# A two-layer graph network on one core: edge values in a ring, twelve gather buffers instead of eight, and some loads issued from another queue

## The chip, the core and the metric

The kernel runs on one core of one Trainium2 chip. The core has five engines that run their own instruction streams and meet at semaphores: TensorE (PE, matmuls; its weight loads are listed as PEld), VectorE (DVE), ScalarE (ACT), GpSimd (POOL) and SyncE (SP), which here only issues DMAs. ACT, SP and POOL can each issue DMAs; each has a queue of its own (SPq, ACTq and POOLq in the rows). Time is device microseconds of one execution, the median of several.

## The reference

1250 nodes with 512 features, 40000 edges sorted by destination. Layer 0 sums over typed edges, layer 1 is a normalised graph convolution:

```
h = relu(layernorm(x))
weight = einsum('rb,bio->rio', w_comp, bases)      # 32 types, 8 bases
msg = (h @ weight[type])[src] * edge_weight
x = x + segment_sum(msg, dst) + h_bias
h = relu(layernorm(x))
h = h @ W.T + b
x = x + relu(segment_sum(norm * h[row], col))      # with self loops, norm from degrees
```

## The kernel before

**Tiles.** The destinations fall into 20 tiles of 64 nodes (NTI), taken in pairs in a fixed order (TORDER). The edges of a tile are cut into slots of 128; there are SL = 335 slots. Of slot s the kernel needs the 128 source rows, two fp16 parts of 512 values and 128 more columns that help count edges (ROW = 1152 values, 2304 bytes a row). They are gathered from a table in HBM (rows_layer0), which the setup writes.

**Gathers.** POOL issues one indirect DMA per slot (line 722) into one of UN = 8 buffers (gath). From slot 8 on it waits for s_used: PE has finished slot s-8. Before slot 5 it waits once for s_cols, since setup values of DVE lie in the later buffers.

**Edge values.** For each edge eight values are needed (its weight times w_comp of its type, one per base). They are made in 42 groups of 8 slots (VB). SP loads the types of a group as rows (line 579, four small DMAs, a ring of three buffers), DVE turns them into a one-hot tile (one_hot_types, line 1087), PE looks the values up (look, line 1404), DVE adds and scales (lines 1094, 1098), ACT casts the high half into val (val_hi, line 782), DVE subtracts the low half (line 1104). All 336 slots have their own place in val. For batches of up to four slots (BATCHES) DVE then spreads the values over the destination window (select, lines 1141 to 1147), in a ring of three batches (sel).

**PE.** For each slot PE runs twelve narrow matmuls (edges, line 1501) into four PSUM banks of a tile and one for the counts (line 1507), which ends the slot and raises s_used. When a tile is done, ACT and DVE flush it (lines 830, 1225, 833) to fp16 parts and PE may not start the next tile's banks before. When both tiles of a pair are flushed, PE has 96 matmuls of 512 columns with the split bases (product, line 1521), then a transpose (turn, line 1530) and a projection with W1 (project, line 1541). After the last slot follow the last products and layer 1's aggregation (line 1595).

**What sets the order.** All engines walk the same list of slots. STEPS[s] says what other work stands behind slot s. PROD[s] says which product matmuls do; they are put between the narrow ones of the next slot. PROD comes from a planner (place_products) that adds up modelled times of gathers, of PE and of the wait for a free buffer, s - UN, and gives each slot some products, 14 where a tile ends, so that they are there to run while the flush goes on.

**The setup.** The bases (8 of 1 MB), W1 (1 MB) and the biases are loaded by SP. ACT squares each base and W1 as they land (squares_of, line 797), for a bound: STEPS puts bases 5 to 7 and W1 behind slots 0 to 3. Behind slot 7 PE transposes the sums (columns_of(1), line 1376), DVE makes the scales from them (scales), and from slot 10 on ACT and DVE split one base every three slots (split_base, lines 841 and 1261). SP's order here is: bases 0 to 4, table rows (line 594), types of groups 0 to 2, bases 5 to 7 (line 558), the two biases (600, 601), W1 (626), types of groups 3 to 5, and x (623).

A general path for inputs that aren't sorted stands in If blocks on each engine; it isn't run here.

## Time and profile before

| | us |
|---|---|
| median of 3 runs | 630.19 (628.79 to 630.42) |
| span of the profiled execution | 625.8 |
| median minus span | 4.4 |

| engine | busy us | share of the span | instructions |
|---|---|---|---|
| PE | 496.4 | 79% | 5824 |
| PEld | 317.0 | 51% | 5824 |
| DVE | 328.6 | 52% | 929 |
| ACT | 151.9 | 24% | 272 |
| POOL | 352.2 | 56% | 473 |

The profile gives one execution, instruction by instruction, from the first to the last instruction of any engine; that is the span. A time of its own around the span isn't given for that execution, so the span is set beside the median. In the slices each digit is a share in tenths. "PEclk" is the clock granted to PE, as a share of 2.4 GHz; its other level is 1.2 GHz. In the order of time a row gives start, duration, engine, line, operation and tiles, and in brackets how long the engine idled before it and what ended that. A matmul's busy time overlaps its neighbours', since their ends are modelled. Names of tiles are those of the memory, so where setup values lie in another tile's place, the row names that tile: base loads go to room_b, W1 to u_t.

### The profile page before, as it was taken

To read this page: it belongs to the slowest core of one execution; us is meant where nothing else is said; L and a number is where in the kernel's file an instruction comes from. 1 tells how busy PE (TensorE), PEld (TensorE's weight loads), DVE (VectorE), ACT (ScalarE), POOL (GpSimd) and SP (SyncE) were. 2 spreads that over 40 slices of the span, in tenths; PEclk is the share of its full clock that TensorE was granted. 3 is DMA by queue.
4 is the path that set the end of the run, shared out by engine and by line. 5 is a ranking of instruction groups with operands and counts; after the bars stand their busy time and mean duration, and the time that the engine had idled before them with its cause. 6 is when DMAs were issued, how large, how long until landed. Compare 5 with 4: busy or idle time off the path is not lost.

```text
span 625.8 us, 15841 instructions
## 1 busy us (share of the span) xinstructions
PE 496.4 (79%) x5824; PEld 317.0 (51%) x5824; DVE 328.6 (52%) x929; ACT 151.9 (24%) x272; POOL 352.2 (56%) x473
## 2 busy tenths in 40 slices
PE   3031445598999899999999998999897876889996
PEld 1020334356666556666656665566564554545443
DVE  7898038885665446636655556645542221544121
ACT  3392234532222122211322202203210000341021
POOL 3334536786676776766747757677677777200000
PEclk9665657599999999999999999999997977789999
DMA  9896965557786887886858868778788788323042
GB/s 283 306 362 216 391 161 150 166 152 211 217 278 202 255 259 205 256 262 175 272 153 252 258 189 262 222 235 273 210 250 261 216 234 240 118 68 102 2 98 68
DMA packets 53427, 132.82 MB, mean 212 GB/s; under 512 B 12173, under 2 KB 18174, under 8 KB 53350
## 3 DMA queue, kind: packets, MB, share of 16 engines
q0 software_dynamic: 27040, 99.60, 53.1%
q1 hardware_dynamic: 25356, 30.99, 15.9%
q8 instruction: 57, 0.93, 0.6%
q10 hardware_dynamic: 954, 1.13, 0.6%
q14 instruction: 20, 0.16, 0.1%
HBM read 120.58 MB, written 11.10 MB: 210 GB/s over the span
## 4 chain that ended last, share of the span: by engine, by line
PE 52%; DMA 14%; DVE 12%; issue 8%; ACT 5%; POOL 5%; SPq 3%; ACTq 1%; POOLq 0%; DVEq 0%
PE PS L1521 22%; PE PS L1501 16%; DMA gath<-rows_layer,srcs 9%; PE PS L1595 7%; POOL gath L722 5%; PE PS L1541 4%; DMA types<-types_by_slot 2%; SPq L579 2%; DVE room_b L1225 2%; ACT room_b L841 2%; DVE zt L1225 1%; DMA edge_records<-room_c 1%; DVE room_b L1261 1%; DMA w1t<-edge_records,w1t 1%; PE PS L1507 1%
## 5 line engine op out<-in xcount | busy, mean ns | idle before, releaser
L722 POOL DMA_INDIRECT gath<-rows_layer,srcs x335 | 335.7, 1002 | 165.1 <-issue 84.8
L1501 PE MATMUL PS<-sel,gath 128*128 128x48 f16 (+7 forms) x4020 | 299.1, 207 | 52.8 <-DMA gath<-rows_layer,srcs 21.8
L1501 PEld LDWEIGHTS PS<-sel,gath 128*128 128x128 f16 x4020 | 235.4, 103 | 163.9 <-issue 86.6
L1521 PE MATMUL PS<-room_b,zt 128*128 128x512 f16 x480 | 168.6, 392 | 1.5 <-DVE sel L1147 1.0
L1521 PE MATMUL PS<-room_b 128*128 128x512 f16 (+1 forms) x480 | 151.7, 384 | 2.0 <-DMA gath<-rows_layer,srcs 1.8
L1141 DVE TENSOR_TENSOR masks<-iota_n,dloc 128x24 bf16<-128x24 f32 (+12 forms) x92 | 17.9, 194 | 96.6 <-issue 58.8
L1507 PE MATMUL PS<-oh_ad,gath 128*128 128x30 bf16 (+7 forms) x335 | 65.1, 194 | 0.0
L782 ACT CAST val<-val_f 128x64 f16<-128x64 f32 x42 | 11.0, 262 | 201.8 <-DVE val_f L1098 196.8
L1521 PEld LDWEIGHTS PS<-room_b 128*128 128x128 f16 (+1 forms) x480 | 47.8, 105 | 16.8 <-DMA gath<-rows_layer,srcs 2.1
L1521 PEld LDWEIGHTS PS<-room_b,zt 128*128 128x128 f16 x480 | 45.2, 100 | 8.6 <-issue 2.2
L1147 DVE TENSOR_TENSOR sel<-masks,val 128x192 f32<-128x192 bf16 (+12 forms) x92 | 38.6, 420 | 0.0
L1507 PEld LDWEIGHTS PS<-oh_ad,gath 128*128 128x128 bf16 x335 | 34.6, 103 | 3.1 <-issue 2.6
L1595 PE MATMUL PS<-zt,room_c 128*128 128x512 f16 (+1 forms) x160 | 36.2, 379 | 0.0
L1094 DVE TENSOR_REDUCE val_f<-PS 128x64 f32<-128x192 f32 x42 | 14.9, 356 | 36.0 <-PE PS L1404 34.2
L1404 PE MATMUL PS<-wparts,oh_t 128*128 128x96 bf16 x84 | 11.0, 215 | 27.0 <-DVE oh_t L1087 25.1
L1225 DVE SCALAR_TENSOR_TENSOR room_b<-PS,room_b 128x512 f16<-128x512 f32 x40 | 24.8, 684 | 12.8 <-ACT room_b L830 12.8
L830 ACT ACTIVATE room_b<-PS 128x512 f16<-128x512 f32 x40 | 20.6, 600 | 38.3 <-PE PS L1507 35.8
L1143 DVE TENSOR_TENSOR oh_ad<-iota_n,code 128x120 bf16<-128x120 f32 (+12 forms) x92 | 29.7, 322 | 0.2 <-issue 0.2
L1225 DVE SCALAR_TENSOR_TENSOR zt<-PS,zt 128x512 f16<-128x512 f32 x40 | 24.8, 683 | 9.3 <-ACT zt L830 9.3
L1541 PE MATMUL PS<-w1t,hT_t 128*128 128x512 f16 (+1 forms) x120 | 27.6, 379 | 1.4 <-DVE val_f L1094 1.4
L833 ACT CAST room_c<-c_i 128x320 f16<-128x320 int32 (+1 forms) x40 | 16.1, 450 | 46.1 <-DVE c_i L1231 46.1
L1595 PEld LDWEIGHTS PS<-zt,room_c 128*128 128x128 f16 (+1 forms) x160 | 16.0, 100 | 18.2
(202 smaller groups left out, 409.9 us busy)
## 6 DMA issues: line engine op xcount, KB each, us to landing
room_b<-in_L_gnn_bases_dram SPq DMA_DIRECT2D x8, 1024.0 KB, 9.3
gath<-rows_layer,srcs POOLq DMA_INDIRECT x335
types<-types_by_slot SPq DMA_DIRECT2D x168, 16.0 KB
x_t<-x_base SPq DMA_DIRECT2D x19, 128.0 KB
u_t<-in_x_dram SPq DMA_DIRECT2D x9, 256.0 KB, 6.2
x_base<-u_t SPq DMA_DIRECT2D x9, 256.0 KB
x_layer<-x_t SPq DMA_DIRECT2D x18, 128.0 KB
u_t<-x_layer SPq DMA_DIRECT2D x18, 128.0 KB, 2.7
```

Source lines behind the costliest of these rows:

```text
L722: pool.indirect_dma_start(out=gath[:, s % UN, :], out_offset=None, in_=tab0_d[:, :], in_offset=bass.IndirectOffsetOnAxis(ap=srcs[:, s:s + ...
L830: a.activation(zt[q % 2][:, 0, f, :, TN * h:TN * (h + 1)], zbank(f), ACT.Copy, scale=ZDOWN).then_inc(s_hi, 1)
L833: a.copy(C[:, HA * k:HA * (k + 1), at:at + n], c_i[:, k, :].rearrange("p (a d) -> p a d", d=TN)[:, :, 0:n]).then_inc(s_cst, 1)
L1141: v.tensor_tensor(mask, iota_n[:, 0:w].unsqueeze(1).to_broadcast([P, k, w]), dloc[:, s:s + k].unsqueeze(2).to_broadcast([P, k, w]), ALU.is ...
L1143: v.tensor_tensor(oh_ad[:, there, 0:k, 0:HA * w], iota_n[:, 0:HA * w].unsqueeze(1).to_broadcast([P, k, HA * w]), code[:, s:s + k].unsqueez ...
L1147: v.tensor_tensor(sel[:, there, 0:k, 0:NB * w].rearrange("p k (b d) -> p k b d", b=NB), mask.unsqueeze(2).to_broadcast([P, k, NB, w]), val ...
L1225: v.scalar_tensor_tensor(lo, zbank(f), ZDOWN, hi, ALU.mult, ALU.subtract).then_inc(s_lo, 1)
L1501: mm(there, gath[:, s % UN, D * t + P * f:D * t + P * (f + 1)], sel_parts[:, here, k, 0:NB * w, u], start=first and t == 0 and u == 1, sto ...
L1507: mm(there, oh_r[:, s % UN, :], oh_ad[:, here, k, 0:HA * w], start=first, stop=True, skip_group_check=True).then_inc(s_used, 1)
L1521: last = mm(PS[0:r, PBANK[q], :], zt[q % 2][:, t, f, b, 0:r], base_hl[:, b, u, f, :], start=(m == 0), stop=(m == NM - 1))
L1541: last = mm(PS[0:r, MB, :], hT_t[:, s, f, 0:r], w1t[:, t, f, :], start=(f == s == t == 0), stop=(f == FT - 1 and s == 1))
L1595: return mm(PS[0:r, FBANK[j], :], there, u_part(i, t)[0:ROWS[i], :], start=first, stop=True, skip_group_check=not first)
```

## The change

**Sizes.** UN goes from 8 to 12: a gather waits for the slot twelve before it. GSET = 7 takes the place of 5 as the slot before which POOL waits for s_cols. val keeps 48 slots (six groups of eight, VR = 6) instead of 336; that frees the room for the four buffers. ACT waits, before it casts group v (from 6 on), until the last selection that reads group v-6 is done (s_sel). A batch may not run over the end of the ring, and there are 94 instead of 92. Setup values that lay in val move to b1_t, to room_c and to the later gather buffers. Some pairs of semaphores become one that counts.

**Queues.** The loads of bases 5 to 7 and of both biases leave SP and are issued by ACT behind its last table cast. The load of W1 leaves SP too, and ACT issues it, with the same wait for the table rows (s_tab0), behind the first three casts of values.

**Planner.** Its code is the same and reads UN. Up to product row 5 nearly nothing moves; row 6 ends at slot 243 instead of 240, row 7 at 277 instead of 271, row 8 at the same slot 335.

```diff
-    UN = 8
+    UN = 12
+    GSET = 7
...
-    BATCHES = [(s, min(BQ, S0[r] + SLOTS[r] - s), r) for r in range(NTI) for s in range(S0[r], S0[r] + SLOTS[r], BQ)]
+    VB, VR = 8, 6
+    VS = VB * VR
+    BATCHES = []
+    for r in range(NTI):
+        s = S0[r]
+        while s <= LAST[r]:
+            k = min(BQ, LAST[r] + 1 - s, VS - s % VS)
+            BATCHES.append((s, k, r))
+            s += k
...
-        val = sb("val", [P, SLV, NB], f32)
+        val = sb("val", [P, VS, NB], f32)
...
-        squares = val[:, :, :].rearrange("p t b -> p (t b)")
-        junk = squares[:, SLV * NB - FT * D // 2:].bitcast(bf16)
+        squares = b1_t
+        junk = room_c[:, TZ * D:TZ * D + FT * D // 2].bitcast(bf16)
...
+        SELECTED = [1 + max(n for n, (s, k, r) in enumerate(BATCHES) if s // VB <= v) for v in range(NVAL)]
...
-            for n in range(BEARLY, NB):
-                load_base(n)
-            sp.dma_start(hb_t[:, :], h_bias.rearrange("(p d) -> p d", p=1).to_broadcast([P, D])).then_inc(s_bias, 16)
-            sp.dma_start(b1_t[:, :], b1.rearrange("(p d) -> p d", p=1).to_broadcast([P, D])).then_inc(s_bias, 16)
...
-            sp.wait_ge(s_tab0, 16 * (NT + 3))
-            sp.dma_start(w_in, W1.rearrange("(c p) i -> p c i", p=P)).then_inc(s_win, 16)
...
-                if s == 5:
+                if s == GSET:
                     pool.wait_ge(s_cols, 1)
                 gather(s)
...
                     high(i - 1)
             high(NT - 1)
 
+            for n in range(BEARLY, NB):
+                act.dma_start(base_in[:, n + 2, :, :], bases[n, :, :].rearrange("(f p) o -> p f o", p=P)).then_inc(s_bin[n], 16)
+            act.dma_start(hb_t[:, :], h_bias.rearrange("(p d) -> p d", p=1).to_broadcast([P, D])).then_inc(s_bias, 16)
+            act.dma_start(b1_t[:, :], b1.rearrange("(p d) -> p d", p=1).to_broadcast([P, D])).then_inc(s_bias, 16)
+
             def val_hi(v):
                 act.wait_ge(s_valf, v + 1)
+                if v >= VR:
+                    act.wait_ge(s_sel, SELECTED[v - VR])
...
+            act.wait_ge(s_tab0, 16 * (NT + 3))
+            act.dma_start(w_in, W1.rearrange("(c p) i -> p c i", p=P)).then_inc(s_win, 16)
```

On SP, the first place, behind the last table row (the rows between belong to the path that isn't run). Before:

```order
L594 DMA rows_layer<-room_c 98x1024
L579 DMA types<-types_by_slot 32x256 x8
L558 DMA room_b<-in_L_gnn_bases_dram 128x4x512 x3
L600 DMA hb_t<-in_L_gnn_h_bias_dram 128x512
L601 DMA b_t<-in_L_gnn_b_dram 128x512
L604 TENSOR_LOAD flag
L604 ISA x2
...
L626 DMA u_t<-in_L_gnn_W_dram 128x4x512
L579 DMA types<-types_by_slot 32x256 x12
L623 DMA x_t<-x_base 64x512 x4
```

Now:

```order
L604 DMA rows_layer<-room_c 98x1024
L589 DMA types<-types_by_slot 32x256 x8
L610 TENSOR_LOAD flag
L610 ISA x2
...
L589 DMA types<-types_by_slot 32x256 x12
L629 DMA x_t<-x_base 64x512 x4
```

The types of groups 3 to 5 (x12) stand directly behind those of groups 1 and 2 (x8). Five loads in front of the flag and W1 behind it are gone.

On ACT, behind the last table cast (the rows left out are the path that isn't run; "val,sq<-room_b" are squares of bases, and "val<-val_f" the casts of values). Before:

```order
L770 CAST room_c<-u_t 98x512
L797 ACTIVATE val,sq<-room_b 128x2048 x5
L782 CAST val<-val_f 128x2x4x8 x3
L805 TENSOR_LOAD flag
L805 ISA x2
...
L806 UNCONDITIONAL_BRANCH
L797 ACTIVATE val,sq<-room_b 128x2048 x3
L797 ACTIVATE val,sq<-u_t 128x2048
L782 CAST val<-val_f 128x2x4x8
```

Now (the lines of the changed kernel: 785 to 787 and 833 are the DMAs, 808 the squares, 793 the casts of values):

```order
L774 CAST room_c<-u_t 98x512
L785 DMA room_b<-in_L_gnn_bases_dram 128x4x512 x3
L786 DMA hb_t<-in_L_gnn_h_bias_dram 128x512
L787 DMA b_t<-in_L_gnn_b_dram 128x512
L808 ACTIVATE room_c,sq<-room_b 128x2048 x5
L793 CAST val<-val_f 128x2x4x8 x3
L816 TENSOR_LOAD flag
...
L817 UNCONDITIONAL_BRANCH
L833 DMA u_t<-in_L_gnn_W_dram 128x4x512
L808 ACTIVATE room_c,sq<-room_b 128x2048 x3
L808 ACTIVATE room_c,sq<-u_t 128x2048
L793 CAST val<-val_f 128x2x4x8
```

The five loads stand between the table and the squares of bases 0 to 4, and W1's load between the three casts of values and the square of base 5.

On PE, in the edge matmuls of slot 246 (12 narrow matmuls, then the count). Before, the first half of the slot:

```order
L1507 MATMUL PS<-oh_ad,gath 128x5x7
L1501 ISA
L1501 MATMUL PS<-sel,gath 128x8x7
L1521 MATMUL PS<-room_b 128x512
L1501 MATMUL PS<-sel,gath 128x8x7 x2
L1501 ISA
L1501 MATMUL PS<-sel,gath 128x8x7
L1521 MATMUL PS<-room_b 128x512
L1501 MATMUL PS<-sel,gath 128x8x7 x2
```

Now, with lines 1516, 1536 and 1522 for 1501, 1521 and 1507:

```order
L1522 MATMUL PS<-oh_ad,gath 128x5x7
L1516 ISA
L1516 MATMUL PS<-sel,gath 128x8x7
L1536 MATMUL PS<-room_b 128x512
L1516 MATMUL PS<-sel,gath 128x8x7 x2
L1516 ISA
L1516 MATMUL PS<-sel,gath 128x8x7 x3
L1516 ISA
L1516 MATMUL PS<-sel,gath 128x8x7 x3
```

Four products stood in that slot, one every three narrow matmuls; now one does. The others come in slots 265 to 277.

## Rows read from the trace of the kernel before

**Rows 1.** The page: busy tenths of PE and its granted clock, 40 slices of 15.6 us
```profile
PE   3031445598999899999999998999897876889996
...
PEclk9665657599999999999999999999997977789999
```

**Rows 2.** Stretches: busy us and instructions by engine, PEclk, DMA share, GB/s
```profile
38.40:44.00 5.60, 3.12 (x19) 2.09 (x16) 5.08 (x20) 5.42 (x6) 0.00 (x0) 0.80 1.05 383
44.00:56.00 12.00, 2.16 (x10) 1.70 (x10) 10.31 (x37) 5.08 (x8) 1.40 (x2) 0.50 0.46 145
...
60.00:84.00 24.00, 6.52 (x91) 6.20 (x91) 2.91 (x11) 6.20 (x7) 10.68 (x11) 0.57 1.02 349
...
97.00:125.00 28.00, 17.67 (x212) 13.31 (x213) 22.58 (x40) 15.00 (x16) 20.45 (x15) 0.68 0.55 157
125.00:200.00 75.00, 68.93 (x885) 45.66 (x884) 49.93 (x132) 20.08 (x40) 53.29 (x52) 1.00 0.73 210
...
364.70:545.00 180.30, 153.23 (x2197) 102.07 (x2195) 76.33 (x243) 24.59 (x57) 126.69 (x132) 0.92 0.78 230
```

**Rows 3.** Order of time, PE, 59:98 (start, us, what, [idle before <-releaser])
```profile
64.67 0.98 PE L1501 MATMUL PS<-sel,gath 128*128 128x80 f16 x12 [8.08 <-issue]
...
84.72 0.32 PE L1404 MATMUL PS<-wparts,oh_t 128*128 128x96 bf16 x2 [13.40 <-DVE oh_t L1087]
...
85.88 0.40 PE L1376 MATMUL PS<-ident,sq 128*12 128x128 f32 x1
```

**Rows 4.** Order of time, DVE, 50:97: the one-hot types
```profile
53.84 0.29 DVE L1087 TENSOR_SCALAR oh_t<-types,rel 128x256 bf16<-128x256 bf16 x1 [0.24 <-DMA types<-types_by_slot]
...
84.29 0.28 DVE L1087 TENSOR_SCALAR oh_t<-types,rel 128x256 bf16<-128x256 bf16 x1 [21.38 <-DMA types<-types_by_slot]
```

**Rows 5.** Order of time, the sync queue's issues, 40:100
```profile
54.29 1.54 SPq L558 DMA_DIRECT2D room_b<-in_L_gnn_bases_dram  x3
...
56.56 1.30 SPq L601 DMA_DIRECT2D b_t<-in_L_gnn_b_dram  x1
...
60.54 14.85 SPq L579 DMA_DIRECT2D types<-types_by_slot  x12
```

**Rows 6.** Order of time, ACT, 36:90
```profile
37.34 1.12 ACT L770 CAST room_c<-u_t 128x512 f16<-128x512 f32 x2
...
53.39 0.26 ACT L782 CAST val<-val_f 128x64 f16<-128x64 f32 x1 [4.65 <-DVE val_f L1098]
...
57.95 0.26 ACT L782 CAST val<-val_f 128x64 f16<-128x64 f32 x1 [2.26 <-DVE val_f L1098]
59.75 1.91 ACT L797 ACTIVATE val<-room_b 128x2048 bf16<-128x2048 f32 x1 [1.53 <-DMA room_b<-in_L_gnn_bases_dram]
...
83.56 1.91 ACT L797 ACTIVATE val<-u_t 128x2048 bf16<-128x2048 f32 x1 [6.37 <-DMA u_t<-in_L_gnn_W_dram]
```

**Rows 7.** Order of time, PE, 360:366: a projection, and a slot end
```profile
361.11 2.75 PE L1541 MATMUL PS<-w1t,hT_t 128*128 128x512 f16 x12
...
364.50 0.18 PE L1507 MATMUL PS<-oh_ad,gath 128*128 128x40 bf16 x1
```

**Rows 8.** Order of time, POOL: three gathers
```profile
54.29 0.96 POOL L722 DMA_INDIRECT gath<-rows_layer,srcs  x1 [17.46 <-issue]
...
364.95 0.94 POOL L722 DMA_INDIRECT gath<-rows_layer,srcs  x1 [2.43 <-PE PS L1507]
...
536.74 0.95 POOL L722 DMA_INDIRECT gath<-rows_layer,srcs  x1 [0.30 <-issue]
```

**Rows 9.** Waits of PE, 136:364.7 and 364.7:545 (total, times, longest)
```profile
PE PS L1501 <- DMA gath<-rows_layer,srcs: 3.0, 5, 1.2
...
PE PS L1501 <- DMA gath<-rows_layer,srcs: 18.8, 28, 1.5
```

**Rows 10.** Order of time, PE, 122:127: product matmuls on both sides of a clock rise
```profile
123.73 0.63 PE L1521 MATMUL PS<-room_b,zt 128*128 128x512 f16 x1
...
125.58 0.38 PE L1521 MATMUL PS<-room_b,zt 128*128 128x512 f16 x1
```

43 lines of the change are left out of this document (21 added, 22 removed).

## The prediction

> **What bounds the kernel now.** I read the slices of the page first, for where TensorE (PE) is not busy, then the stretches, then each engine's order of time at the places found, then the waits.
>
> The slices [rows 1] show three parts. Up to about 125 us (slice 8) PE is idle or at its lower clock. Then PE reads 9 almost throughout, to about 400 us. After that it reads 8, 7 and 6 now and then until 545 us, and the end is PE work again. The stretches [rows 2] put numbers on it: PE is busy 68.93 of 75 us in 125:200, but 153.23 of 180.3 in 364.7:545.
>
> *The start.* PE begins the edge matmuls at 64.67 us, does seven slots in 6.65 us, and then waits 13.40 us for the one-hot types (line 1087) [rows 3]. VectorE (DVE) makes that tile as soon as its rows land, after 21.38 us of idling on the transfer types<-types_by_slot [rows 4]. The sync queue shows why: it issues bases 5 to 7 (line 558) and both biases from 54.29 to 57.86 us, then W1, and the twelve small types transfers (line 579) take 14.85 us to issue from 60.54 us behind them [rows 5]. At the same time ScalarE (ACT) waits for these bases one after the other: the square of base 5 starts at 59.75 us, two more follow after the same kind of wait, and W1's at 83.56 us after 6.37 us of waiting [rows 6]. The second column maximum on PE (line 1376, 85.88 us) needs that last square, and everything that splits the bases hangs on it. So two things end together at 84 to 86 us: the types and W1. The DMA engines are full (1.02) in 60:84, but only 0.46 busy in 44:56 [rows 2]: the queue had nothing in it then.
>
> *The later part.* GpSimd (POOL) issues one gather per slot. One takes 0.96 us (126.69/132, [rows 2]) and 0.30 us lie between two when no buffer is waited for, so 1.26 us. PE's need is uneven. Twelve matmuls of 512 columns take 2.75 us in a projection, 0.23 us each [rows 7]; an ordinary slot with two products (0.46 us) and its thirteen narrow matmuls stays below 1.26 us, the first slot after a flush has fourteen products, 3.2 us, and a projection adds 2.75. In such a place POOL runs until the eight buffers are full and stops (2.43 us before the gather at 364.95 us, [rows 8]); then PE runs faster than 1.26 us a slot, eats the lead, and waits for landings. These waits are 3.0 us in 136:364.7 and 18.8 us in 364.7:545 [rows 9].
>
> **The change part by part.**
>
> *1. Bases 5 to 7 and the biases from ACT's queue.* ACT issues them after its last cast of the table, at 38.5 us instead of 54.29 us on the sync queue [rows 5, 6]. There the five took 3.6 us to issue; on ACT that moves the squares of bases 0 to 4, which end 4.65 us before the cast at 53.39 us, from 48.7 to 52.3 us. The cover is that idle time [rows 6], so it costs nothing; if ACT's queue blocked as the sync queue did at 60.54 us, it would cost up to 8 us.
>
> The bytes: 3.1 MB of bases and 0.5 MB of biases. The engines move 383 KB/us when full and moved 145 in 44:56 [rows 2], so 12 x 238 KB = 2.9 MB of room lie there. The bases then land at about 56 to 58 us. But the sync queue's own 3.3 MB in 40:56 (4 x 383 + 12 x 145 KB) include the table rows that every gather needs. If two full queues share the engines evenly, these take 3.3 MB / 191 KB/us = 17.3 us from 40 us, that is until 57.3 us. Now the first gather goes out at 54.29 us [rows 8]. Bounds: no delay, if the sync queue is served first, and 9 us, if ACT's 3.6 MB go first. I take +3.0 us: first gather at 57.3 us. Types group 1, behind the same rows, moves DVE's chain by as much or a bit more: its tile is made at 53.84 us after a short wait for the landing [rows 4], then at 57.6, and the third cast of values on ACT (57.95 us, [rows 6]) moves to 61.8 us. The first selections, which end just ahead of PE's start now, end at 65 us.
>
> *2. W1 from ACT.* ACT issues it after the third cast of the setup at 62 us and has it out at 63 us, some 3 us later than the sync queue does now, but with no base ahead. One MB with gathers beside it (128 rows of 2304 bytes, 295 KB, per 1.26 us: 234 KB/us, which leaves 149 KB/us, or 191 in an even share) takes 5.5 to 7 us and some 2 us until the first bytes move: it lands at 70.8 us in place of 83.5. Squares 5 to 7 fit ahead of it (three times 2.1 us from 63.2; a square is 1.91 us and its read 0.19). W1's square ends at 72.9 us.
>
> *3. The types transfers* are issued from 54.3 us, right behind groups 1 and 2; groups 3 to 5 are there by 62 us, and the 13.40 us wait goes. What is late next is PE itself with the gathers: they start 3.0 us later, but land sooner, since no bases fill the engines beside them, so PE starts when the selections are there, at 65.5 us, takes the same 6.65 us for seven slots, and 1.1 us for the look-up and slot 7 (84.72 to 85.88 us now, [rows 3]): 73.2 us. So both inputs of line 1376 are ready at about 73.0 us instead of 85.88: **-12.9 us**. Behind it stands the same chain at the same lower clock (scales, base splits, flush), in which PE waited for DVE and not for gathers, so the shift is carried whole into the later part. Ends: -15.5 (no delay of the tables) and -7 us (tables 6 us later).
>
> *4. Twelve gather buffers.* Up to 364.7 us they can save at most the 3.0 us of landing waits there [rows 9], since POOL then stands four slots further ahead at each congested place. I take **-3.0 us**. For the rest take the slot whose end, at 364.68 us, freed the buffer of the gather at 364.95 us [rows 7, 8]. 132 gathers start in 364.7:545, so that is number 203 and the slot is number 195. With twelve buffers the same slot end frees the buffer of gather 207. Now: from that slot's end to the last gather (number 334, at 536.74 us) pass 172.06 us. Then: 0.27 + 127 x 1.26 = 160.3 us, and about 0.5 us for one more stop, at the next flush with a projection (slots 224 and 225), where POOL's and PE's times come within half a microsecond. So **-11.2 us**. The sum of the two, 14.2 us, is below the 21.8 us of landing waits, as it must be. Past the last gather nothing changes. Ends: -9 us (1.28 us a gather) and -17 us.
>
> *5. The planner* takes twelve buffers into its sum and puts products later: base product row 6 ends at slot 243 instead of 240, row 7 at 277 instead of 271; the count of products is the same. Since POOL's rate bounds there, moving PE work within the stretch costs nothing; if it holds a flush or projection back, 1 us. The cover is the lead of twelve slots.
>
> *6. The ring of six value groups.* ACT now waits, before casting group v, for the selections of group v-6. At that step DVE has selected some 30 slots beyond that group, so nothing queues there: 0. Two batches more (94 for 92) are some 2 us of DVE work, and DVE is busy 76 of 180 us in the last stretch [rows 2]: 0.
>
> **Sum.** 12.9 + 3.0 + 11.2 = 27.1 us off the profiled span: 625.8 to 598.7 us. The median of the runs lies 4.4 us above that span, which the change doesn't touch: 630.2 - 27.1 = **603.1 us**.
>
> **The rivals.**
> *A. The queue is not the limit.* The DMA engines are full from 56 to 84 us, so bytes rather than order would set when W1 lands; then W1 comes at its old time, the start gains nothing, and only the buffers pay: 630.2 - 14.2 = 616 us. For: 1.02 in 60:84. Against: 0.46 in 44:56. In a sentence by itself: the Trainium skill, page "DMA: Bandwidth & Descriptors", section "Issuing engines are not separate DMA queues", says that DMAs started from different engines run on the same 16 DMA engines, interleave, and save only the time of issuing. By that rule taken alone the time would be this rival's; the trace agrees on the shared engines but shows them half idle for 12 us, so an earlier issue has room. A milder form (tables 6 us later, early gain 7 us) gives 609 us.
> *B. The gathers gain nothing from more buffers*, because gathers issued earlier land later (the first slot began 10.4 us after its gather was issued, when the engines were full, [rows 3, 8]) or POOL's pace falls to 1.30 us: the later gain drops to 3 to 8 us, 607 to 612 us.
> *C. Slower, by the clock.* PE has its lower clock (1.2 GHz; 0.50 to 0.68 granted on average) until 125 us and the full one (2.4 GHz) from there [rows 2]. A product matmul occupies 0.63 us at the lower level and 0.38 at the higher [rows 10], so a slot of 1.0 us becomes 1.66. If the compressed start left PE too thinly busy for the rise, each further slot at the lower clock would cost 0.66 us. It needs 41 such slots, so a rise only some 68 us later than the same work now sees it, to lose the 27.1 us; with 60 slots the time is 643 us. Against it: the order of the work ahead of the rise is the same and PE's waits there are shorter.
> *D. Both gains are larger* (tables not delayed, lead of four more slots at every flush): 593 to 598 us.
> *E. The change doesn't do what it says:* the four extra buffers are never filled ahead and the types still wait: 629 to 631 us.
>
> **How the numbers follow.** Forecast 0.60; A 0.14 (its mild form included); B 0.12; D 0.09; C 0.03; E 0.02. The likeliest gives 603.1 us. The range reaches into A's mild form, B and the edge of D: 596 to 613 us. About 0.3% (1.9 us) is what a measurement can tell from no change: faster 0.95, within 0.3% 0.02, slower 0.03.
>
> **What would show it.** The profile after should have: the bases' DMAs on ACT's queue near 38.5 us and squares 5 to 7 with no wait between them; the first gather at 57 us; W1's square ending near 73 us; no wait of line 1087 for types above 1 us; line 1376 near 73 us; the DMA share in 44:56 above 0.9. Later: POOL's stops before flushes 195 and 225 remain, those in between vanish; gathers follow each other at 1.26 us to the last one near 510 us; PE's waits for landings fall from 21.8 to about 8 us. It is wrong if the first gather moves beyond 60 us, if W1 lands after 76 us, or if POOL's pace per gather rises.

## The result, and the profile after

The changed kernel takes 607.18 us (median of 4 runs, 605.49 to 609.06) against 630.31 us (628.79 to 632.82) for the kernel before on the same chip: a ratio of 0.9644, 95% interval 0.9607 to 0.9681. It is 23.1 us faster. Forecast were 603.1 us and a gain of 27.1. Of the profiled executions, the span falls from 625.8 to 605.4 us.

In every run that lists both, the time is 1.8 to 1.9 us above the span. By that the profiled execution of the kernel before, of 625.8 us, would have taken about 627.7 us. It was some 2.6 us faster than the median, while that of the changed kernel (607.27 us) was an ordinary one. The traces therefore differ by 20.5 us where the medians differ by 23.1, and where in the kernel those 2.6 us lie, they can't tell.

The page of the changed kernel, as [rows 1], in slices of 15.1 us:

```profile
PE   3031256688999999999999999998997966989996
...
PEclk9655567689999999999999999999999887799999
```

Slices 5 to 7 are fuller (5, 6, 6 for 4, 5, 5), slice 4 is emptier. PE's clock stays at its higher level from slice 9 on (135.0 us; before from 125.3 us). The late stretch that read 8, 7 and 6 now and then reads 9 more often. The stretches, as [rows 2] (us; busy us and instructions of PE, its weight load, DVE, ACT, POOL; granted clock, DMA share, GB/s):

```profile
44.00:56.00 12.00, 1.84 (x8) 1.56 (x8) 8.52 (x31) 10.16 (x11) 0.00 (x0) 0.59 1.06 404
...
66.00:74.00 8.00, 4.06 (x52) 3.73 (x52) 3.35 (x15) 5.01 (x6) 6.17 (x7) 0.50 1.00 291
74.00:84.00 10.00, 6.85 (x95) 5.98 (x96) 2.99 (x15) 2.15 (x3) 7.56 (x9) 0.67 0.99 347
...
356.40:525.00 168.60, 148.95 (x2191) 99.59 (x2189) 75.16 (x241) 23.26 (x55) 122.49 (x128) 0.94 0.79 239
```

The free 12 us of the DMA engines are filled (0.46 to 1.06). From 66 to 74 us they are busy all the time too, but move only 291 GB/s. The order of time on PE, as [rows 3]:

```profile
68.21 0.98 PE L1516 MATMUL PS<-sel,gath 128*128 128x80 f16 x12 [5.97 <-DVE sel L1161]
...
71.81 1.14 PE L1516 MATMUL PS<-sel,gath 128*128 128x80 f16 x12 [0.72 <-DMA gath<-rows_layer,srcs]
...
75.70 1.14 PE L1516 MATMUL PS<-sel,gath 128*128 128x80 f16 x12 [2.71 <-DMA gath<-rows_layer,srcs]
...
80.86 0.27 PE L1391 MATMUL PS<-ident,sq 128*12 128x128 f32 x1 [0.79 <-ACT room_c L808]
```

The 13.40 us wait for the one-hot types is gone. But PE starts at 68.21 us, 3.5 us later than before, then waits twice for gathers, and the second column maximum (now line 1391) comes at 80.86 us, 5.0 us before the 85.88 of [rows 3] and not 12.9. ACT, as [rows 6], shows the new issues and the wait for W1:

```profile
37.91 1.20 ACTq L785 DMA_DIRECT2D room_b<-in_L_gnn_bases_dram  x2
39.14 2.34 ACTq L786 DMA_DIRECT2D hb_t<-in_L_gnn_h_bias_dram  x1
41.52 2.47 ACTq L787 DMA_DIRECT2D b_t<-in_L_gnn_b_dram  x1
44.09 1.91 ACT L808 ACTIVATE room_c<-room_b 128x2048 bf16<-128x2048 f32 x1 [5.65 <-issue]
...
64.52 0.38 ACTq L833 DMA_DIRECT2D u_t<-in_L_gnn_W_dram  x1
...
78.72 1.91 ACT L808 ACTIVATE room_c<-u_t 128x2048 bf16<-128x2048 f32 x1 [7.52 <-DMA u_t<-in_L_gnn_W_dram]
```

The gathers on POOL, as [rows 8]: the first one, number 207 and the last one.

```profile
60.35 0.96 POOL L726 DMA_INDIRECT gath<-rows_layer,srcs  x1 [23.64 <-issue]
...
356.65 0.94 POOL L726 DMA_INDIRECT gath<-rows_layer,srcs  x1 [2.44 <-PE PS L1522]
...
517.04 0.95 POOL L726 DMA_INDIRECT gath<-rows_layer,srcs  x1 [0.31 <-issue]
```

The first is 6.1 us later than before, the last 19.7 us earlier. PE's waits for landings, as [rows 9], in 100:525, in total, times and longest (all of them lie behind 356.4 us):

```profile
PE PS L1516 <- DMA gath<-rows_layer,srcs: 11.0, 15, 2.0
PE PS L1536 <- DMA gath<-rows_layer,srcs: 1.6, 3, 0.7
```

To see where the time goes, take the end of each slot, the end of its count matmul on PE (line 1507 before, 1522 after). The table below gives, for some slots, how much earlier (-) or later (+) than in the kernel before a slot ends, in us:

```
kernel                                  slot 13   slot 93   slot 195  slot 334  span
changed kernel                           -5.2      -7.4      -8.3     -18.8    -20.5
twelve buffers alone (e1)                +3.0      +0.9      -0.1     -10.6    -12.2
loads moved alone (e2)                   -7.3      -7.3      -5.3      -5.7     -5.7
```

The first line splits the gain: 5.2 us at the start, 3.1 more up to slot 195, 10.5 behind that slot, 1.7 in the tail.

Each line comes from one execution, so small differences in it mean little. Six kernels have the same program up to the first gather (the changed one and the runs with x_base held back, with ten buffers, with the old plan, and the two that only move W1's step). Their first gathers lie between 59.54 and 61.33 us, and slot 13 of the changed kernel, of the one with ten buffers and of the one with the old plan ends at 94.02, 93.64 and 93.22 us.

The tail's 1.7 us are not a gain of the change. From the end of slot 334 on, the same work takes 82.3 us in six of the fourteen traces and 80.6 us in the other eight, whatever the edit, and the granted clock goes with it. The kernel before is one of the six. Its trace has 3.4 us at the lower clock (1.2 GHz) from 555.3 us on, and the changed kernel's is at 2.4 GHz (1.00) at the same work (stretches as above, the kernel before first):

```profile
555.00:560.00 5.00, 5.00 (x18) 2.57 (x17) 2.70 (x4) 4.79 (x9) 0.00 (x0) 0.66 0.22 61
```

```profile
536.00:541.00 5.00, 5.00 (x27) 2.98 (x26) 2.70 (x4) 4.58 (x8) 0.00 (x0) 1.00 0.17 49
```

The opposite happens once near slot 38, where the changed kernel's trace is at the lower clock from 131.6 to 135.0 us and that of the kernel before is not:

```profile
131.00:136.00 5.00, 5.00 (x26) 2.35 (x27) 4.82 (x14) 1.71 (x5) 4.00 (x4) 0.66 0.67 185
```

### The profile page after: what moved, and what is told of

It reads as the page before. It is cut to its first block, busy times and chain, and to the rows that moved or that the text cites. A ratio compares the mean times of both kernels' runs of the same rounds, so it can differ in the third digit from the quotient of the medians.

```text
span 605.4 us, 15887 instructions
## 1 busy us (share of the span) xinstructions
PE 491.5 (81%) x5824; PEld 314.6 (52%) x5824; DVE 328.2 (54%) x935; ACT 151.7 (25%) x272; POOL 351.3 (58%) x473
## 4 chain that ended last, share of the span: by engine, by line
PE 59%; DVE 14%; DMA 12%; issue 6%; ACT 6%; POOL 1%; ACTq 1%; SPq 0%; DVEq 0%
PE PS L1536 26%; PE PS L1516 19%; PE PS L1610 7%; DMA gath<-rows_layer,srcs 6%; PE PS L1556 4%; DMA u_t<-in_L_gnn_W_dram 2%; ACT room_b L855 2%; DVE room_b L1240 2%; DVE zt L1240 2%; DMA w1t<-edge_records,w1t 1%; DVE room_b L1276 1%; DMA types<-types_by_slot 1%; DMA edge_records<-room_c 1%; PE PS L1522 1%; ACT room_b L844 1%
## 5 line engine op out<-in xcount | busy, mean ns | idle before, releaser
L1516 PE MATMUL PS<-sel,gath 128*128 128x48 f16 (+7 forms) x4020 | 294.8, 207 | 44.6 <-DVE zt L1240 14.9
L1536 PE MATMUL PS<-room_b,zt 128*128 128x512 f16 x480 | 170.4, 395 | 2.6 <-DVE sel L1161 2.0
L1536 PE MATMUL PS<-room_b 128*128 128x512 f16 (+1 forms) x480 | 149.6, 380 | 1.6 <-DMA gath<-rows_layer,srcs 1.1
L1155 DVE TENSOR_TENSOR masks<-iota_n,dloc 128x24 bf16<-128x24 f32 (+14 forms) x94 | 18.1, 193 | 85.2 <-issue 55.9
L1161 DVE TENSOR_TENSOR sel<-masks,val 128x192 f32<-128x192 bf16 (+14 forms) x94 | 39.0, 415 | 0.0
L1157 DVE TENSOR_TENSOR oh_ad<-iota_n,code 128x120 bf16<-128x120 f32 (+14 forms) x94 | 30.1, 320 | 0.2 <-issue 0.2
```

The costliest lines, as they stand in the source:

```text
L1155: v.tensor_tensor(mask, iota_n[:, 0:w].unsqueeze(1).to_broadcast([P, k, w]), dloc[:, s:s + k].unsqueeze(2).to_broadcast([P, k, w]), ALU.is ...
L1157: v.tensor_tensor(oh_ad[:, there, 0:k, 0:HA * w], iota_n[:, 0:HA * w].unsqueeze(1).to_broadcast([P, k, HA * w]), code[:, s:s + k].unsqueez ...
L1161: v.tensor_tensor(sel[:, there, 0:k, 0:NB * w].rearrange("p k (b d) -> p k b d", b=NB), mask.unsqueeze(2).to_broadcast([P, k, NB, w]), val ...
L1516: mm(there, gath[:, s % UN, D * t + P * f:D * t + P * (f + 1)], sel_parts[:, here, k, 0:NB * w, u], start=first and t == 0 and u == 1, sto ...
L1536: last = mm(PS[0:r, PBANK[q], :], zt[q % 2][:, t, f, b, 0:r], base_hl[:, b, u, f, :], start=(m == 0), stop=(m == NM - 1))
```

## The experiments

Times are medians of 4 runs; each ratio is against the kernel before on the same chip. Edits are against the changed kernel unless said otherwise.

### One half of the change at a time

The buffers alone put the loads back on SP:

```
-            act.dma_start(base_in[...], bases[n, ...])      # bases 5 to 7, and both biases
-            act.wait_ge(s_tab0, 16 * (NT + 3))
-            act.dma_start(w_in, W1...)
+            sp: bases 5 to 7 and both biases behind load_types(2), W1 behind s_tab0
```

> The changed kernel with bases 5 to 7, the two biases and W1 issued from SP's queue at the places they had in the kernel before: twelve gather buffers and the ring of value groups alone. Theory 1 (start and buffers are separate terms that add; the start is worth the 5.0 us by which the step at the end of W1's square came earlier, the rest of the 23.1 us is the buffers'): 612 us, the last gather about 5 us later than in the changed kernel. Rival (the earlier start passes into a wait further on, so that it is worth little at the end): 607 to 609 us. Second rival (the buffers gain less without the early start, since the first stops of POOL then come elsewhere): over 615 us.

Measured: 615.08 us, ratio 0.9781 (0.9756 to 0.9806), 14 us faster than before. By its number this stands at the second rival's edge, 3 us from the additive theory, but for another reason than that rival's. At slot 13 this kernel is 3.0 us *behind* the kernel before (table above), because W1, with more gathers in flight beside it, takes 27.8 us from issue to landing (a query of the transfers; KB, median us to landing), and its square starts at 86.50 us, not 83.56 ([rows 6]):

```profile
u_t<-in_L_gnn_W_dram SPq DMA_DIRECT2D x1, 1024.0 KB, 27.8
```

```profile
86.50 1.91 ACT L809 ACTIVATE room_c<-u_t 128x2048 bf16<-128x2048 f32 x1 [9.16 <-DMA u_t<-in_L_gnn_W_dram]
```

The buffers explain the size: by 78 us this kernel has issued 19 gathers and the kernel before 15. Four gathers are 1.2 MB, which is 3.1 us at 383 KB/us.

From slot 13 on it gains 13.6 us (+3.0 to -10.6), just as much as the changed kernel (-5.2 to -18.8). So what twelve buffers bring behind the start doesn't depend on how the start went.

The loads alone are the same moves made in the kernel before, with its eight buffers (in place of 12) and its undivided value tile.

> The kernel before with only the loads moved: bases 5 to 7, biases and W1 from ScalarE's queue, eight gather buffers as before. Theory 1 (terms add): 630.3 less 5.0, 625 us. Rival (the rest of the 5 us is eaten by later stops for buffers): 628 to 630 us. Second rival (twelve gathers in flight crowd out W1 at 64 to 76 us; with eight there is less in flight): W1 lands some us before the 78.8 us of the changed kernel, and the step at W1's square comes near 76 us, for 621 us.

Measured: 623.60 us, ratio 0.9917 (0.9893 to 0.9941), 5.2 us faster. At slot 13 it leads by 7.3 us, more than the changed kernel, as the second rival said (W1's square starts at 76.79 us, against 78.72). Of that 1.6 us go again by slot 334. So twelve buffers cost 3.0 us in the start beside the old order. Beside the moved loads the difference is 2.1 us in these two traces, and 1.3 us if the run with the old plan is taken for the changed kernel. Its cause isn't shown: when W1 lands, both kernels have issued as many gathers (13 by 76.8 us and 15 by 78.7 us in each). The two halves measured alone give 14 + 5 = 19 us, both together 22 to 23. Of the rest, 0.9 us come from the start by slot 13, and 1.6 us are what the moved loads lose again with eight buffers and keep with twelve.

### What slows W1 and the first gathers

```
+            sp.wait_ge(s_win, 16)
             load_x(0)
             load_x(1)
```

> The changed kernel with the first two tiles of x_base (4 loads of 128 KB) held back on SP until W1 has landed. Between 66 and 74 us the DMA engines were busy (0.88 to 1.05) while they moved only 220 to 330 GB/s, and 4608-byte packets took 215 to 252 ns there, against 195 ns at 74 to 80. Theory 1 (the loads of x_base are what slows the packets; without them 380 GB/s): the 1 MB of W1 and the first seven gathers land 3 to 5 us earlier, W1 at 74 to 76 us, the step at W1's square at about 77, the time 603 to 604 us. Rival 1 (W1's own packets are slow, or its queue, whatever runs beside): W1 still near 78, 607 us. Rival 2 (only the 0.5 MB count, at 380 GB/s 1.4 us): W1 near 77.5, 606 us.

Measured: 603.46 us, ratio 0.9589 (0.9555 to 0.9624), about 3.5 us faster than the changed kernel by the ratios, though the two intervals overlap a little. The trace bears theory 1 out. The stretches of this kernel, and below them those of the changed one:

```profile
68.00:70.00 2.00, 1.56 (x23) 1.57 (x24) 0.76 (x3) 1.91 (x3) 1.39 (x2) 0.50 1.01 374
70.00:74.00 4.00, 2.62 (x46) 2.37 (x43) 0.74 (x4) 1.38 (x2) 3.09 (x4) 0.84 0.99 355
```

```profile
68.00:70.00 2.00, 1.79 (x26) 1.80 (x27) 0.71 (x3) 1.91 (x3) 1.44 (x2) 0.50 1.01 323
70.00:74.00 4.00, 2.27 (x30) 1.93 (x27) 0.64 (x4) 1.20 (x2) 3.09 (x4) 0.50 1.05 307
```

About the same busy share moves 374 and 355 GB/s where it moved 323 and 307; over all of 66:74 it is 336 against 291. W1 lands after 10.5 us instead of 14.2, its square begins at 75.18 us, and the column maximum comes at 77.33 us. Slot 13 ends 3.6 us sooner than in the changed kernel (2.8 us sooner than with the old plan). Slot 334 ends 5.0 us sooner, in part because this trace has no lower clock near slot 38, and the span only 3.2 us, since it has the slower tail. The 0.5 MB alone would be 1.4 us at 374 GB/s.

Then the biases behind W1, on the same queue:

```
-            act.dma_start(hb_t ...); act.dma_start(b1_t ...)     # behind the bases
             act.dma_start(w_in, W1...)
+            act.dma_start(hb_t ...); act.dma_start(b1_t ...)
```

> The changed kernel with the two bias loads (0.5 MB in packets to 128 partitions each) behind W1 on ScalarE's queue, not ahead of the squares. Theory 1 (the table rows, and with them the first gather, are late because ScalarE's queue takes half of the engines from 44 to 57 us): 0.5 MB less ahead of them brings the first gather from 60.35 to about 59.0 us, and ScalarE's squares begin 4.8 us earlier; W1 is issued 1.3 us earlier; gain 1 us or so, 606 us. Rival (the time to the first gather is set by ScalarE's issue of 6.5 us and not by bytes): the first gather near 60, nothing gained, 607 us. Rival 2: the biases then meet the first gathers at 66 to 74 us and cost what they saved, 607 to 608 us.

Measured: 606.07 us, ratio 0.9633 (0.9608 to 0.9659), which can't be told from the changed kernel. The first gather comes 1.3 us sooner, as theory 1 says. One trace wouldn't show that, given the 59.54 to 61.33 us of the six kernels with the same start. But the three runs with the biases out of the way have it at 58.30, 59.06 and 59.60 us, on average 1.3 us before the average of those six:

```profile
59.06 1.00 POOL L726 DMA_INDIRECT gath<-rows_layer,srcs  x1 [22.34 <-issue]
```

But slot 5 ends at 78.1 us (77.9 in the changed kernel) and slot 13 at the same time to 0.1 us: the 0.5 MB now lie beside the gathers. That is rival 2.

Both sets of loads out of the way:

```
-            act.dma_start(hb_t ...); act.dma_start(b1_t ...)
-            load_x(0); load_x(1)
+                if s == 14:
+                    sp.wait_ge(s_used, 14)
+                    load_x(0); load_x(1); and both biases
```

> The changed kernel with both bias loads and the first two tiles of x_base issued on SP only after slot 13's edges, ahead of nothing that needs them before slot 59; bases 5 to 7 and W1 stay on ScalarE's queue. Theory 1 (until slot 12 the start is paced by what the DMA engines have to move, and slowed by the loads of x_base: holding the latter back gave 3.7 us, and the 0.5 MB of biases ahead of the first gather 1.3 us at that gather): slot 12's edges end at 82 to 83 us against 86.0, the time 601 to 602 us. Rival 1 (slots 4 to 12 are paced by POOL's 1.26 us a gather and the time to land, not by bytes): the biases' 1.3 us are gained as well, 602 us, but 12 gathers still land more than 7 us after their issue. Rival 2 (the loads of x_base cost the same wherever they lie): slots 14 to 24 lose what slots 4 to 12 gained, 605 to 607 us.

Measured: 603.34 us, ratio 0.9577 (0.9524 to 0.9630). Slot 12 ends at 82.7 us, as expected, and slots 14 to 24 don't lose it, but slot 13 gains only 3.1 us, so the biases add nothing to what holding x_base back brings (603.46). Rival 2 is out. The 1.3 us of the biases at the first gather don't reach slot 13, and why they don't is left open.

### How many buffers, and the planner

```
-    UN = 12
+    UN = 10
-    GSET = 7
+    GSET = 5
```

> The changed kernel with ten gather buffers instead of twelve (and five in place of seven slots ahead of the set-up values). Theory 1 (after slot 195 the end is the end of that slot plus one gather per 1.263 us for the gathers that its buffers did not yet hold): gather 205 in place of 207 is the first one freed by slot 195's end, 129 in place of 127 follow, 2.5 us later at the end; and some of the 1 to 3 us up to slot 195 is lost: 610 to 612 us. Rival (two buffers more or fewer change only the few stops of 1 to 3 us that POOL still has): 608 us. Second rival (each buffer beyond eight also slows the start, where fewer gathers in flight land sooner): the start gains 1 us and the time is 609 us.

Measured: 610.53 us, ratio 0.9705 (0.9651 to 0.9758), 3.8 us above the changed kernel by the ratios, whose intervals overlap. The trace is theory 1 to the gather. The one after the stop at slot 195's end is number 205, and its successors follow without a gap to the last:

```profile
357.69 0.94 POOL L726 DMA_INDIRECT gath<-rows_layer,srcs  x1 [2.48 <-PE PS L1522]
...
520.80 0.94 POOL L726 DMA_INDIRECT gath<-rows_layer,srcs  x1 [0.30 <-issue]
```

That is 163.1 us for 129 gathers, 1.264 us each. The changed kernel has 160.4 us for 127. Up to slot 195 ten buffers lose 1.4 us of the 3.1.

Then the planner, the part that decides between which slots the product matmuls lie:

```
-                t_g = max(t_g, t_done[s - UN] + 2.0 if s >= UN else 0.0) + GATHER
+                t_g = max(t_g, t_done[s - 8] + 2.0 if s >= 8 else 0.0) + GATHER
-                until = max(t_g, t_done[s + 1 - UN] + 2.0 if s + 1 >= UN else 0.0) + GATHER + LAND
+                until = max(t_g, t_done[s + 1 - 8] + 2.0 if s + 1 >= 8 else 0.0) + GATHER + LAND
```

> The changed kernel with twelve buffers, but the planner of the products counting with eight as before, so that products lie between the edge slots as in the kernel before (99 slots differ). Theory 1 (the moved products are worth nothing: fewer small pieces are a matter of 0 to 1 us): 606 to 608 us. Rival (the planner's wider look carries part of the gain behind slot 195, where the two kernels' products lie differently): 610 us or more.

Measured: 605.95 us, ratio 0.9626 (0.9571 to 0.9682): no difference from the changed kernel. Against that kernel it is 1.5 us ahead at slot 237, 1.9 behind at 247 and 3.7 ahead at 300: PE's place within the stretch is free while POOL's rate sets the end.

### Is it W1's wait, or what comes with it?

```
-        SQ_SETUP, SC_AT, BS_AT, WT_AT = BEARLY, 7, 10, 38
+        SQ_SETUP, SC_AT, BS_AT, WT_AT = BEARLY, 12, 15, 38
```

> The changed kernel with the step that needs W1's square moved from behind slot 7 to behind slot 12 (the base splits from 10, 13, ... to 15, 18, ...). Theory 1 (gathers 4 to 12 landed 1.1 to 3.4 us ahead of their edges' ends, so what the gathers and W1 compete for sets the start and W1's wait alone costs 0.8 to 1.5 us): slot 12 ends near 85 us against 86.0, 606 us. Rival (the forecast's reading, W1's chain alone sets the start): the edges of slots 8 to 12 are free of it and slot 12 ends near 83 us, 604 us. Second rival (the step then meets flush 0 behind slot 12 and delays it): 608 us or more.

Measured: 605.32 us, ratio 0.9617 (0.9565 to 0.9668); against the changed kernel's 0.9644 no more than a hint. Yet the trace moved a lot. Slot 12 ended 2.1 us sooner, between theory and rival, and slot 13 6.3 us sooner, because base split 0 and its low half no longer stood ahead of flush 0 on ACT and VectorE: PE waits 1.49 us before slot 13 and not 5.84. Then, at slot 38, 4.2 us of it went. ACT shows why:

```profile
128.81 2.06 ACT L844 ACTIVATE room_b<-PS 128x512 f16<-128x512 f32 x4 [3.83 <-DVE room_b L1276]
```

Flush 2, behind slot 37 (ended at 122.6 us), writes where the base inputs lay, so it waits for the last of VectorE's low halves of the bases (the changed kernel's trace has 2.4 us of this wait). My edit had pushed these back by five slots. The remedy is to put the splits closer together:

```
-        SQ_SETUP, SC_AT, BS_AT, WT_AT = BEARLY, 7, 10, 38
+        SQ_SETUP, SC_AT, BS_AT, WT_AT = BEARLY, 12, 15, 38
-            STEPS[BS_AT + 3 * n].append(("bsplit", n))
+            STEPS[BS_AT + 2 * n].append(("bsplit", n))
```

> The changed kernel with only the step that needs W1's square behind slot 12 and the base splits at slots 15, 17, ... 29; the loads as in the changed kernel. Theory 1 (as in the run with the splits three slots apart, but nothing lost at slot 38): slot 38 ends 5 to 6 us before the changed kernel's 136.4, 601 to 602 us. Rival (slot 38's loss is another wait, not the splits): slot 38 again only 2 us ahead, 605 us.

Measured: 603.37 us, ratio 0.9579 (0.9537 to 0.9620). Slot 38 ends 5.8 us ahead of the changed kernel, as theory 1 wants, and slot 334 4.4 us; the time is 1 to 2 us above it.

And with both loads deferred as in the run above:

> The kernel with the deferred x_base and bias loads, and in addition the step that needs W1's square behind slot 12 with the base splits at slots 15, 17, ... 29. Theory 1 (with the step moved alone slot 13 ended 6.3 us earlier and slot 37 too, and 4.2 us of it went at slot 38, where flush 2 waited for the last base split on VectorE, which my later splits had delayed; two slots apart they are done in time): the gain of the moved step stays, 4 to 6 us, beside the 3 to 4 us of the deferral, of which 1 to 2 us are the same: 598 to 600 us. Rival 1 (the splits crowd VectorE between slots 15 and 30 and the selections come late): 602 to 604 us. Rival 2 (both edits shorten the same stretch, so they don't add): 603 us.

Measured: 601.36 us, ratio 0.9546 (0.9505 to 0.9587), the fastest version found, about 6 us below the changed kernel. It is 9.8 us ahead of the changed kernel at slot 13, but only 5.0 at slot 25 and 6.4 at the end. So rival 1 is in it too: with five splits between slots 13 and 24, VectorE is late for flush 1, and PE waits for it 9.06 us at slot 25, where it waited 5.51 us in the run with the splits three slots apart (each kernel's order of time on PE, this one first):

```profile
108.16 0.78 PE L1518 MATMUL PS<-sel,gath 128*128 128x80 f16 x6 [9.06 <-DVE zt L1242]
```

```profile
105.60 0.78 PE L1516 MATMUL PS<-sel,gath 128*128 128x80 f16 x6 [5.51 <-DVE zt L1240]
```

### The other queue, or the earlier time?

First ScalarE's queue without the earlier time:

```
-            act.dma_start(... bases 5 to 7, biases ...)          # behind the last cast of the table
             act.wait_ge(s_tab0, 16 * (NT + 3))
+            act.dma_start(... bases 5 to 7, biases ...)
             act.dma_start(w_in, W1...)
```

> The changed kernel with bases 5 to 7 and the biases still on ScalarE's queue, but issued only when the table rows have landed, ahead of W1 on the same queue. It tells the other queue apart from the earlier time. Theory 1 (what counts is when the bytes move, not who issues them): the first gather is back at 54 us, the bases meet the first gathers as in the kernel with the twelve buffers alone, W1 lands at 84 to 88 us, and the time is that kernel's, 612 to 616 us. Rival (a queue of their own brings the bases and W1 through sooner even beside the gathers): W1 lands before 80 us, 605 to 608 us.

Measured: 621.08 us, ratio 0.9864 (0.9815 to 0.9912). The rival is out, and theory 1 has the side right and the size wrong: 14 us above the changed kernel and 5 above my bound. The same 14 us are there at the end of slot 8 and at slot 334. The first gather is at 54.80 us as expected, but W1 is there only at 92.5. ACT issues behind its three casts, from 59.39 us, and spends 11.1 us on the six issues (6.5 + 0.4 in the changed kernel), beside gathers all the while. Against the run with the buffers alone (615.08 us), which has these loads on SP, the time is 5 us longer: W1 is issued 9.1 us later and lands 6.0 us later. How much of that is ACT's slow issue, and how much W1's place behind all five other loads, no run separates. Two of the issues, W1's square, and on PE the column maximum:

```profile
63.15 4.63 ACTq L832 DMA_DIRECT2D b_t<-in_L_gnn_b_dram  x1
67.81 2.69 ACTq L833 DMA_DIRECT2D u_t<-in_L_gnn_W_dram  x1
...
92.52 1.91 ACT L804 ACTIVATE room_c<-u_t 128x2048 bf16<-128x2048 f32 x1 [3.28 <-DMA u_t<-in_L_gnn_W_dram]
```

```profile
94.66 0.37 PE L1391 MATMUL PS<-ident,sq 128*12 128x128 f32 x1 [19.53 <-ACT room_c L804]
```

Then the earlier time without ScalarE's queue:

```
-            for n in range(1, BEARLY):
+            for n in range(1, NB):
                 load_base(n)                                   # SP, ahead of the edge types and table rows
-            act.dma_start(base_in[...], bases[n, ...])          # bases 5 to 7
```

> The changed kernel with bases 5 to 7 issued from SP's queue as early as can be, straight behind base 4 and so ahead of the edge types, the table rows and the types' loads; biases and W1 stay on ScalarE's queue. It tells the early time apart from the other queue. Theory 1 (only the bytes that have to move before the first gather count, whoever issues them: 3 MB more, as in the changed kernel): the first gather near 60 us, ScalarE's squares begin 1.5 us earlier, 606 to 608 us. Rival (what the second queue buys is that the edge types and the table rows don't stand behind the 3 MB in one queue): the edge types' first tile lands some 8 us later than in the changed kernel, the first gather at 63 us or later, 610 us or more.

Measured: 608.86 us, ratio 0.9667 (0.9628 to 0.9705): its interval overlaps that of the changed kernel, between the two expectations. SP does get late, as the rival says: it issues the first types at 52.19 us, 6.5 us later than the changed kernel's 45.71. Yet the first gather comes at 61.40 us, only 1.05 us later, and slots 13 and 334 end 0.5 and 0.6 us later, which is about the scatter. Another 1.7 us of the span are the slower tail.

The first gather:

```profile
61.40 0.96 POOL L726 DMA_INDIRECT gath<-rows_layer,srcs  x1 [24.68 <-issue]
```

What these two runs say together: the gain of the start comes from moving 3 MB at a time when the engines were half idle. Which queue issues the three bases makes a difference of 1.7 us in the medians, which the intervals and the tail's clock leave open to be nothing. The biases and W1 stayed on ScalarE's queue in both runs, so for them this isn't shown.

## Why the prediction was right, and where it was wrong

The time lies in the range, and both mechanisms are in the trace, but the likeliest value came near for mixed reasons. The late gain was right in place and size. The early gain was 7.7 us too large. The step that failed most is W1's landing (part 2), and beside it the first gather (part 1) and the pace of the first slots (part 3). Two of the prediction's own three signs of being wrong came true: the first gather moved beyond 60 us (60.35), and W1 landed after 76 us (78.69). Part of the miss was made up by luck: 1.7 us of clock in the tail. Another part is the 2.6 us by which the medians differ more than the two traces, and these stay unexplained.

**1. The bases and their bytes: right in kind, mis-sized.** The issue is where it was put (37.45 us instead of 38.5), the squares of bases 5 to 7 follow each other without waits, and the DMA share in 44:56 is 1.06. ACT's issue took 6.5 us and not 3.6 (2.34 and 2.47 us for the biases alone); the cover held, the first cast moved by 1.3 us only (53.39 to 54.69). What failed is "+3.0: first gather at 57.3 us". It came at 60.35, +6.1 us. That is nearer to "ACT's bytes go first": (3.3 + 3.6) MB at 383 KB/us from 40 us on end at 58.0 us, and the last rows need to land. In 44:56 the packet records give ACT's queue 2.8 MB and SP's 2.1, so the share was not even. A reason stands in SP's order of time, a landing inside its chain. SP doesn't issue the types' first tile until the edge types that it wrote itself have landed, and the later table rows stand behind that:

```profile
37.41 1.29 SPq L595 DMA_DIRECT2D types_by_slot<-h_t  x3
38.75 2.03 SPq L604 DMA_DIRECT2D rows_layer<-zt  x4
45.71 1.79 SPq L589 DMA_DIRECT2D types<-types_by_slot  x4
...
48.01 2.80 SPq L604 DMA_DIRECT2D rows_layer<-room_c  x5
```

This tile's issue was at 42.36 us before. So SP issued nothing from 40.78 to 45.71 us, and ACT's queue had the engines. It seems no price of its own: with the same tile issued at 52.19 us and the bases in front, the first gather came only 1.05 us later. What counts is the bytes ahead of the gather, as far as the runs tell: without the 524 KB of biases it came 1.3 us sooner on average, which is about 410 KB/us.

**2. W1: the step that failed most.** Forecast: issue 62, landing 70.8, square ended 72.9 us. Measured: issue 64.52 (the third cast, behind the late types), landing after 14.2 us and not 8.8, square from 78.72. I had divided 383 KB/us between W1 and the gathers. The engines were busy but moved 291 GB/s in 66:74, and the run with the loads of x_base held back shows that these make up 3.7 us of the 5.4. The prediction never moved those loads in its account; SP reached them at 63.54 us once the types no longer blocked it (75.44 before), right into W1 and the first gathers. It also put the price of twelve buffers in the start at nothing. In the old order they put four more gathers, 1.2 MB, ahead of W1's landing, and slot 13 ended 3.0 us later. With the moved loads the difference is 1.3 to 2.1 us, and there the number of gathers is no explanation; its cause stays open.

**3. The types: right, but not the end of it.** The 13.40 us wait is gone. "PE takes the same 6.65 us for seven slots" was wrong: slots 3 to 7 went at the pace of landings. PE waited 0.72 and 2.71 us before slots 3 and 4, and the semaphores of these five gathers give 7.5 to 10.1 us from issue to landing. PE's start was 2.7 us later than forecast as well: the first selections came at 68.2 us and not at 65, behind table rows and types that were late themselves. So what bounded the start was again bytes, and by the time PE reached line 1391 W1 cost it only 0.79 us more. Sum for parts 1 to 3: -5.0 us at line 1376 (now 1391), -5.2 at slot 13, against -12.9. The lower end (-7) was too narrow.

The mild form of rival A, with table rows 6 us late and 7 us of early gain, described this start best, and its time of 609 us is nearer to 607.2 than the forecast's. Rival B's 607 to 612 us hold the time too, but not its mechanism (below). The milder A's mechanism holds in part. The Trainium skill, page "DMA: Bandwidth & Descriptors", section "Issuing engines are not separate DMA queues", says that DMAs of different engines run on the same 16 DMA engines and that only the time of issuing is saved. The last two experiments agree: 1.7 us between the two queues for the bases at the same early time, and 14 us between an early and a late issue from the same queue. The plain form of rival A, no gain in the start, fell: the idle 12 us were real.

**4. The buffers: right, place by place.** Up to slot 195 the forecast was -3.0 us and the trace has -3.1. That close a match is partly luck: the three traces with twelve buffers and no lower clock near slot 38 in which nothing else was moved there (x_base held back, both loads deferred, old plan) gain 3.8 to 3.9 us between slots 13 and 195. From slot 195's end to the last gather -11.2 was forecast and -11.4 came (172.06 to 160.66 us); 0.9 us of it went again between that gather and the end of slot 334, which leaves -10.5, and the forecast had said that nothing changes there. The step was: the same slot end that freed gather 203 now frees gather 207. PE's count matmul of slot 195 ends at 356.38 us and the gather of [2.44] starts at 356.65, the same 0.27 us; then 127 gathers of 1.263 us. Of the extra stop at slots 224 and 225, for which 0.5 us were allowed, 0.16 us came: POOL idles 0.46 us before gather 237, which needs slot 225's buffer, and not the usual 0.30. PE's landing waits at the narrow matmuls fell from the 21.8 us of [rows 9] to 11.0, not to 8; with those at product matmuls they fell from 24.1 to 12.6 us. The run with ten buffers is the best proof, since it moves the last gather by what the formula gives. Rival B falls with it: POOL's time for a gather is 0.957 us (122.49/128) against 0.960.

**5 and 6. Planner and ring: 0, as forecast.** The old plan gave 605.95 us. The ring was not tried by itself, so its 0 is argued and not measured; no wait of ACT for selections is among the waits of the trace.

**The sum.** 5.2 + 3.1 + 10.5 = 18.8 us to slot 334 and 1.7 us in the tail, 20.5 us between the traces against 27.1 forecast; the medians differ by 23.1 us. The gain between the traces is thus 6.6 us short, that between the medians 4.0 us.

**The clock (rival C).** It didn't make the change slower, but it did play a part. The prediction put it as low until 125 us and full from there. In the trace of the kernel before it was high from 101.4 to 111.6 us already, and low for 27 us in all behind slot 195 and for 3.4 us in the tail. In the changed kernel it rose at 117.9 us and not at 125.3, but fell once more from 131.6 to 135.0 us. That cost 1.8 us at slot 38 against the run with the old plan (from slot 37's end to slot 38's end 7.4 and 5.6 us), of which 0.8 us are left at slot 195. The tail without a stretch at the lower clock is worth 1.7 us. Together the clock favours the changed kernel's trace by about 0.9 us.

## What to carry to other kernels

A transfer moved to an idle stretch gains at most what that stretch can hold, and here little or nothing by the name of its queue. Follow every transfer that the removed wait had held back (here 0.5 MB of x_base, 12 us earlier), and count more buffers as more bytes that can be in flight ahead of the one transfer that the start waits for (3.0 us in the old order).

When a producer runs at a fixed rate behind an uneven consumer, find the last place at which it stops for a buffer: from there the end is that moment plus the remaining count times the rate, and each further buffer moves it by one period. From slot 195's end to the last gather this gave the late gain to within 0.2 us, and the step to ten buffers as well (2.7 us more, 2.5 expected).

A step moved behind a wait may sit ahead of something else that the same engine must do. Here 4.2 of 6.3 us went again 25 slots later.

Before a difference of 1 or 2 us between two traces is put down to an edit, compare the granted clock at the same work. Here the same tail took 80.6 or 82.3 us, and that was as much as several of the effects looked for.

## What the runs showed of the hardware

- Nearly the same busy share of the DMA engines (0.99 to 1.05) moved 323 and 307 GB/s in 68:70 and 70:74 while four loads of 128 KB from x_base to 64 partitions ran beside W1 and gathers, and 374 and 355 without them. In the packet records of these stretches W1's packets of 2 KB took 103 and 117 ns on average with them, 89 and 94 ns without. Whether their source, the 64 partitions or the mixture is the cause was not tried. A DMA share near 1.0 is thus not the full rate.
- A bias load took ACT 0.36 us to issue with nothing ahead of it in its queue (below, the kernel with the bases on SP), and 2.22 to 4.03 us behind three bases at that time (seven traces). Beside gathers the first bias took 1.10 us behind three bases, and the second one 4.63. In the first case SP was issuing seven bases at the time (28.15 to 39.15 us), so the long issues go with what stood in ACT's own queue.

```profile
37.46 0.36 ACTq L784 DMA_DIRECT2D hb_t<-in_L_gnn_h_bias_dram  x1
```

- The tail from slot 334's end took 80.61 to 80.63 us in eight traces and 82.29 to 82.33 us in six, which have 3.4 us at the lower clock some 12 us into it.
